# A vision tower's first stage on one core: zero products at the start, row 1 shared with ScalarE, group 4 in halves

## The reference

```python
concat = (x, x shifted by 4 pixels to the four diagonals)      # 10 channels, zero padded
normed = (concat - mean) * rsqrt(var + 1e-7)                   # over the whole image
y = conv(normed * gamma + beta, W, 8 x 8 patches, stride 8) + b  # 13 x 13 = 169 tokens of 128
h = [cls_tok, y]                                               # 170 tokens
# for each token in turn, memory S starts at memory0:
q, k, v = Wq l, Wk l, Wv l        with l = layernorm(h)
S = S + 0.01 * v k^T ;  h = h + S q
h = h + ffn(layernorm(h))         # ffn adds nothing beyond its input for these values
```

## Time and profile before

| what | value |
|---|---|
| time, median of 3 runs | 217.07 us (217.06 to 217.54) |
| the profiled execution's own time | 217.46 us |
| its span, first to last instruction | 215.6 us |
| TensorE busy | 196.3 us (91%) |
| GpSimd busy | 154.5 us (72%) |
| VectorE busy | 152.3 us (71%) |
| ScalarE busy | 127.7 us (59%) |

### The profile page before, as it was taken

One profiled execution on the slowest core, in us unless ns is written; L12 is line 12 of the kernel. 1 busy time (PEld: TensorE's weight loads), 2 busy tenths in 40 slices (PEclk: granted clock), 3 DMA queues, 4 the chain that ended last, 5 costly groups with the idle time before them and its releaser, 6 DMA issues.

```text
span 215.6 us, 5028 instructions
## 1 busy us (share of the span) xinstructions
PE 196.3 (91%) x1548; PEld 166.9 (77%) x1548; DVE 152.3 (71%) x758; ACT 127.7 (59%) x306; POOL 154.5 (72%) x129
## 2 busy tenths in 40 slices
PE   0699999999999999999999999999999999999720
PEld 0488897886888889788888888899888888888610
DVE  3639694684486675678687597687687687699892
ACT  4215777884443375475756565665665574577982
POOL 1069908899990999969999949938999541455671
PEclk9999999999999999999999999999999999999975
DMA  5999992745022006153053432022012012100356
GB/s 140 388 420 422 422 413 112 217 185 181 0 58 111 2 3 194 30 175 88 3 153 109 125 93 49 5 50 49 11 41 52 16 36 52 28 22 5 80 118 152
DMA packets 17216, 25.90 MB, mean 120 GB/s; under 512 B 1719, under 2 KB 13693, under 8 KB 17062
## 3 DMA queue, kind: packets, MB, share of 16 engines
q1 hardware_dynamic: 16486, 25.41, 36.5%
q10 hardware_dynamic: 704, 0.17, 0.4%
HBM read 19.65 MB, written 5.92 MB: 119 GB/s over the span
## 4 chain that ended last, share of the span: by engine, by line
PE 52%; POOL 15%; DMA 10%; DVE 8%; issue 7%; SPq 4%; ACT 2%; POOLq 0%; DVEq 0%; ACTq 0%
PE conv L575 25%; DMA images<-x_rows 10%; PE vr_ps L623 10%; POOL scaled L469 7%; PE first_ps L633 6%; PE outs L650 6%; POOL rstd L1337 3%; PE turn L608 3%; POOL g_low L1327 2%; DVE state L1007 2%; DVE state L999 2%; SPq L488 1%; PE conv L583 1%; DVE images L1028 1%; POOL rstd L1353 1%
## 5 line engine op out<-in xcount | busy, mean ns | idle before, releaser
L575 PE MATMUL conv<-scaled,wt 128*128 128x256 f32 (+3 forms) x432 | 111.7, 375 | 7.3 <-DMA wt<-weight 6.9
L469 POOL TENSOR_TENSOR scaled<-rows,gam 128x832 f32<-128x832 f32 (+1 forms) x54 | 84.7, 1588 | 17.6 <-DMA rows<-x_windows 17.3
L575 PEld LDWEIGHTS conv<-scaled,wt 128*128 128x128 f32 x432 | 71.7, 193 | 15.3 <-DMA wt<-weight 6.9
L817 ACT ACTIVATE values<-vr_ps,rstd 128x256 f32<-128x256 f32 x76 | 36.0, 473 | 62.8 <-PE vr_ps L623 50.1
L1337 POOL TENSOR_TENSOR rstd<-var,powers 128x8 f32<-128x8 f32 (+2 forms) x20 | 30.3, 1517 | 27.0 <-DVE var L1019 26.9
L999 DVE TENSOR_TENSOR state<-first_ps,state 128x128 f32<-128x128 f32 x76 | 22.1, 291 | 27.6 <-PE first_ps L633 22.2
L825 ACT ACTIVATE images<-images,ln_shift,ln_gain 128x128 f32<-128x128 f32 x80 | 37.3, 489 | 1.5 <-DVE ln_shift L1076 0.7
L623 PE MATMUL vr_ps<-w_high,g_low 128*128 128x256 f32 x77 | 30.8, 400 | 0.8 <-ACT values L817 0.8
L1327 POOL TENSOR_TENSOR g_low<-g_t,g_high 128x512 fp32r<-128x512 f32 x21 | 26.8, 1274 | 4.6 <-ACT g_high L804 4.6
L988 DVE BATCH_NORM_STATS2 ln_stats<-images 128x6 f32<-128x128 f32 x85 | 23.6, 284 | 4.8 <-ACT images L811 4.7
L1007 DVE TENSOR_TENSOR state<-second_ps,state 128x128 f32<-128x128 f32 x76 | 21.5, 282 | 2.1
(11 more groups left out here) (201 smaller groups left out, 273.5 us busy)
## 6 DMA issues: line engine op xcount, KB each, us to landing
rows<-x_windows SPq DMA_DIRECT2D x12, 864.0 KB, 4.8
out<-images SPq DMA_DIRECT2D x40, 128.0 KB, 2.4
images<-x_rows SPq DMA_DIRECT2D x4, 832.0 KB, 14.9
images<-x_rows SPq DMA_DIRECT2D x1, 1040.0 KB, 15.9
images<-x_rows SPq DMA_DIRECT2D x1, 624.0 KB, 20.7
rows<-x_windows SPq DMA_DIRECT2D x1, 448.0 KB, 6.1
gam<-gamma SPq DMA_DIRECT2D x1, 422.5 KB, 6.8
bet<-beta SPq DMA_DIRECT2D x1, 422.5 KB, 9.0
```

The lines of the kernel that those rows point to most:

```text
L469: return eng.tensor_tensor(scaled[:, s, at + skip:at + N], window[:, skip:N], gains.unsqueeze(2).to_broadcast([P, N - skip, B]), ALU.mult)
L575: last = pe.matmul(conv_ps[g % 2][:, at:at + n * B], held, scaled[:, s, a % RING:a % RING + n], start=first, stop=(g < EARLY and s >= TOP ...
L817: act.activation(values[:, t % VALUE_SLOTS].rearrange("p a e -> p (a e)"), vr_bank(t)[:, 0:2 * E], ACT.Identity, scale=rho_of(t)).then_inc ...
```

## The change

- **Opening of TensorE.** Three products of zeros (128 x 512) run before the weights are waited for, and one more after the items of shift 0 of group 0. They write a bank that the next product into it overwrites. The table of gamma comes before that of beta, with the items of shifts 0 and 1 of group 1 between them.
- **Row 0 on VectorE** is scaled in two passes: tokens 0 to 7 of the four shifts, then tokens 8 to 12. The semaphore `scaled_first` counts to 8 instead of 4, and SyncE's load of row 3 waits for all 8.
- **Row 1.** ScalarE scales tokens 13 to 15 of the five shifts (15 instructions of 64 elements) ahead of its work on `center`; GpSimd scales the other ten (640 elements for 832). A new semaphore `scaled_second` tells of the first. SyncE's load of row 4 waits for it too.
- **Group 4 by halves.** All first halves (tokens 32 to 35) of its five shifts, then the second halves: four items before the sums of the statistics, five after, one after L755, and then two items of group 5 (`AHEAD`) that the loop no longer has in step -8.
- **The item table.** `FIRST` gives 4 items to step -8 for 2, the two of them ahead; the rest of the table is dealt out anew. The groups 5, 6, 7, 10, 11, 12 and 17 end one or two steps earlier, and 23 of GpSimd's row scalings stand one step earlier.
- **VectorE's low parts of the tables** (`table_low_ready`) come after the first block of image statistics instead of the second.

```diff
--- before.py
+++ after.py
@@ -95,7 +95,8 @@
 LATE_ITEMS = [item for g in range(EARLY, GROUPS) for item in conv_items(g)]
 LATE_COST = [n for _, _, _, n in LATE_ITEMS]
 
-FIRST = (2, 2, 1, 1, 1, 1, 1, 1)
+AHEAD = 2
+FIRST = (4, 2, 1, 1, 1, 1, 1, 1)
 
 
 def late_item_step(i):
@@ -150,6 +151,7 @@
 ROW_4_TOKENS = {-7: (0, 5), -6: (5, 4), -4: (9, 4)}
 EARLY_TOKENS = TOKENS * EARLY
 CORNER = 3 * N
+SECOND = 2 * TOKENS
 
 
 def pool_scales(r, s):
@@ -436,7 +439,7 @@
         def wait_scaled(eng, s, a, n):
             last = (a + n - 1) // N
             if a // N == 0:
-                eng.wait_ge(scaled_first, s + 1)
+                eng.wait_ge(scaled_first, s + 1 if a < TOKENS else TOP + 1 + s + 1)
             if a + n - 1 == CORNER:
                 eng.wait_ge(corner_scaled, s + 1)
                 last -= 1
@@ -444,6 +447,8 @@
                 eng.wait_ge(scaled_by_scalar, BY_SCALAR.index((last, s)) + 1)
             elif (last, s) in BY_VECTOR:
                 eng.wait_ge(scaled_by_vector, 1)
+            elif 0 < last and a + n <= SECOND:
+                eng.wait_ge(scaled_second, s + 1)
             elif last > 0:
                 eng.wait_ge(scaled_rows, pool_scales(last, s))
 
@@ -457,17 +462,17 @@
             at = (t % PER_GROUP) * E
             return buf[t // PER_GROUP % slots][:, at:at + E]
 
-        def scale_shift(eng, r, s):
+        def scale_shift(eng, r, s, first=0, stop=N):
             offsets = (r if s < 3 else r - 1) % ROW_SLOTS
             right = N + (s - 1) % 2
             window = rows[:, r % ROW_SLOTS, 0:N] if s == 0 else rows[:, offsets, right:right + N]
-            skip = 1 if r * N == CORNER else 0
-            gains = gam_first[:, s] if r == 0 else gam[:, s, r * N + skip:r * N + N]
+            skip = 1 if r * N == CORNER else first
+            gains = gam_first[:, s, skip:stop] if r == 0 else gam[:, s, r * N + skip:r * N + stop]
             if (r, s) == (N - 1, BOTTOM):
                 gains = bottom[:, E:E + N]
             at = r % 2 * N
-            return eng.tensor_tensor(scaled[:, s, at + skip:at + N], window[:, skip:N],
-                                     gains.unsqueeze(2).to_broadcast([P, N - skip, B]), ALU.mult)
+            return eng.tensor_tensor(scaled[:, s, at + skip:at + stop], window[:, skip:stop],
+                                     gains.unsqueeze(2).to_broadcast([P, stop - skip, B]), ALU.mult)
 
         block = ctx.enter_context(nc.Block())
 
@@ -481,6 +486,8 @@
                         sp.wait_ge(scaled_by_vector, 1)
                     if r - 3 >= CORNER // N:
                         sp.wait_ge(corner_scaled, SHIFTS)
+                if r == ROW_SLOTS:
+                    sp.wait_ge(scaled_second, SHIFTS)
                 sp.dma_start(rows[:, r % ROW_SLOTS], x_windows[:, r]).then_inc(row_in[r % ROW_SLOTS], 16)
 
             def load_images(i):
@@ -516,7 +523,7 @@
             load_images(5)
             load_images(6)
 
-            sp.wait_ge(scaled_first, TOP + 1)
+            sp.wait_ge(scaled_first, 2 * (TOP + 1))
             load_row(3)
             load_row(4)
             for blk in range(2):
@@ -588,9 +595,14 @@
                     if a <= item[1] < z:
                         conv(item)
 
+            def conv_fifth(a, z):
+                items = conv_items(EARLY - 1)
+                for item in (items[0::2] + items[1::2])[a:z]:
+                    conv(item)
+
             def late_conv(t, half):
 
-                share = [i for i, st in enumerate(ITEM_STEPS) if st == t]
+                share = [i for i, st in enumerate(ITEM_STEPS) if st == t and i >= AHEAD]
                 mid = (len(share) + 1) // 2
                 for i in share[:mid] if half == 0 else share[mid:]:
                     conv(LATE_ITEMS[i])
@@ -703,15 +715,28 @@
                 reads(LAST)
                 reads(LAST + 1)
 
+            def zero_products(count):
+                for _ in range(count):
+                    pe.matmul(vr_ps[:, 0:PER_GROUP * E], zeros[:], zeros[:].unsqueeze(1).to_broadcast([P, PER_GROUP, E]),
+                              start=True, stop=True, skip_group_check=True)
+
+            pe.wait_ge(zeros_ready, 1)
+            zero_products(3)
             pe.wait_ge(weight_in, 16)
-            conv_shifts(0, 0, SHIFTS)
-            pe.wait_ge(gamma_in, 16)
-            pe.wait_ge(beta_in, 16)
-            for kind, table in enumerate((bet, gam)):
+            conv_shifts(0, 0, 1)
+            zero_products(1)
+            conv_shifts(0, 1, SHIFTS)
+            def table_columns(kind, table):
                 for i in range(SHIFTS):
                     last = pe.matmul(turn_ps[:, kind * PATCHES:kind * PATCHES + PATCHES], wt[:, i], table[:, i], start=(i == 0),
                                      stop=(i == SHIFTS - 1), skip_group_check=True)
-            last.then_inc(columns_done, 1)
+                return last
+
+            pe.wait_ge(gamma_in, 16)
+            table_columns(1, gam)
+            conv_shifts(1, 0, 2)
+            pe.wait_ge(beta_in, 16)
+            table_columns(0, bet).then_inc(columns_done, 1)
             pe.wait_ge(small_in, 16)
             pe.wait_ge(centered, 3)
             pe.matmul(out_ps[:, 0:E], wk_c[:], wq_c[:], start=True, stop=True, skip_group_check=True)
@@ -724,7 +749,7 @@
                 for kind in range(2):
                     last = pe.transpose(ps[0:count, kind * E:kind * E + E], columns[:, kind, blk * P:blk * P + count], small[:, IDENT])
                 last.then_inc(tables_done, 1)
-            conv_shifts(1, 0, SHIFTS)
+            conv_shifts(1, 2, SHIFTS)
             pe.wait_ge(cls_t_ready, 1)
             pe.wait_ge(w_vr_ready, 2)
             pe.matmul(vr_ps[:, 0:2 * E], cls_t[:], w_vr[:], start=True, stop=True).then_inc(vr_done, 1)
@@ -744,24 +769,26 @@
             pe.matmul(first_ps[:, 0:E], values[:, VALUE_SLOTS - 1, 0], values[:, VALUE_SLOTS - 1, 1], start=False,
                       stop=True, skip_group_check=True).then_inc(cls_state_done, 1)
             conv_shifts(3, 0, SHIFTS)
+            conv_fifth(0, 4)
             pe.wait_ge(sums_ready, 2)
             pe.wait_ge(w_low_ready, 1)
             pe.wait_ge(scalar_sums_ready, 3)
             pe.matmul(out_ps[:, 2 * E:2 * E + 2], small[:, SAME], sums[:], start=True, stop=False, skip_group_check=True)
             pe.matmul(out_ps[:, 2 * E:2 * E + 2], small[:, SAME], scalar_sums[:], start=False, stop=True,
                       skip_group_check=True).then_inc(image_sums_done, 1)
-            conv_shifts(EARLY - 1, 0, 2)
+            conv_fifth(4, 9)
             pe.wait_ge(scale_cols_ready, 1)
             pe.matmul(out_ps[:, 0:B], scale_cols[:], small[:, IDENT, 0:B], start=True,
                       stop=True).then_inc(scale_rows_done, 1)
-            conv_shifts(EARLY - 1, 2, 4)
+            conv_fifth(9, 10)
+            for item in LATE_ITEMS[0:AHEAD]:
+                conv(item)
             pe.wait_ge(own_scales_ready, 1)
             pe.wait_ge(early_rows_ready, 1)
             early(0)
             pe.wait_ge(state_ready, 1)
             early(1)
             early(2)
-            conv_shifts(EARLY - 1, 4, SHIFTS)
             pe.matmul(out_ps[:, 0:E], cls_t[:], state[:, STATE_SLOTS - 1, 1], start=True,
                       stop=True).then_inc(out_done, 1)
             for t in range(START, TAIL):
@@ -915,6 +942,12 @@
             act.wait_ge(cls_in, 32)
             act.wait_ge(cls_padded, 1)
             act.copy(cls_t[:, B:P], cls_col[:].to_broadcast([P, B])).then_inc(cls_t_ready, 1)
+            act.wait_ge(gamma_in, 16)
+            act.wait_ge(row_in[1], 16)
+            for s in range(SHIFTS):
+                for t in range(N, SECOND):
+                    last = scale_token(t, s)
+                last.then_inc(scaled_second, 1)
             act.wait_ge(small_in, 16)
             act.wait_ge(ones_ready, 1)
             act.activation(center[:], small[:, IDENT], ACT.Identity, bias=powers[:, 11:12]).then_inc(centered, 1)
@@ -1223,7 +1256,9 @@
                     dve.wait_ge(first_right_in, 16)
                 if s == TOP:
                     dve.wait_ge(first_offsets_in, 16)
-                scale_shift(dve, 0, s).then_inc(scaled_first, 1)
+                scale_shift(dve, 0, s, 0, TOKENS).then_inc(scaled_first, 1)
+            for s in range(TOP + 1):
+                scale_shift(dve, 0, s, TOKENS).then_inc(scaled_first, 1)
 
             dve.wait_ge(small_in, 16)
             for i, w in enumerate((WQ, WK)):
@@ -1258,16 +1293,17 @@
                         else:
                             part = part.rearrange("p r (g q) -> p r g q", q=HALF)[:, :, 0:S // HALF:S // HALF - 1]
                         last_stats = dve.bn_stats(stats[:, 2 * j:2 * j + 2].rearrange("p a b -> p (a b)"), part)
+                if i == 0:
+                    for blk, ps in enumerate((turn_ps, second_ps)):
+                        m = P if blk == 0 else PATCHES - P
+                        dve.wait_ge(table_high_ready, blk + 1)
```

(9 more changed lines are left out.)

1 line of the change is left out of this document (added).

## The result

| | before | after |
|---|---|---|
| median | 217.31 us (217.06 to 217.73, 4 runs) | 215.43 us (215.33 to 215.53, 4 runs) |
| profiled execution, span | 217.46, 215.6 us | 215.34, 213.5 us |
| ratio after / before | | 0.9905 (95%: 0.9891 to 0.992) |

The change makes the kernel 0.95% faster, 1.9 us by the medians and 2.1 us between the two profiled executions. 215.5 us had been predicted.

The account below looks back on a forecast made before the run. TensorE, busy 91% of the span, was taken as the bound. 0.31 + 0.86 + 0.45 = 1.6 us off the profiled 217.46 gives 215.84; less 0.39, its excess over the median, 215.5 us; range 214.7 to 216.9.

Parts of the forecast that it names:

- Part 1: TensorE's opening: zeros end at 6.1, full clock from about 6.93, group 0 ends at 11.5 instead of near 13.9.
- late release: Rival, opening: clock rises only near 10.5, lead 0.25 for 1.07, 0.8 us gained, 216.3 us; chance 0.13.
- The slower rival: Opening: clock stays at or falls back to 1.2 GHz until about 13; +0.9 us, 218.0 us; chance 0.08.
- Part 2: Tables and row 1: `wk_c` ends at 17.5, 1.0 us later; four items done early; lead 1.07 us.
- Part 3: Group 4: sums' product 0.3 late, `early(0)` at 38.1, loop starts with lead 0.31, two group 5 items (0.86) done besides.
- the lead goes into the statistics: Rival, before the sums: lead 0.5, `early` 1.1 late, 0.6 us or less gained, 216.5 to 217 us; chance 0.14.
- Part 4: Loop: 0.86 comes back at steps 11, 23 and 59; GpSimd's earlier scaling (6, 0) gains 0.45; wait near 51 stays.
- The 0.86: Two items of group 5 done ahead, to come back in the loop where the new table has an item less.
- The 0.45 for the wait near 91: Loop: scaling (6, 0) moves into GpSimd's idle time, so TensorE's wait at 91.84 goes; 0.45 us, bounds 0 and 0.6.
- The wait near 51: Loop, TensorE waiting for GpSimd: stays at 0.74; a scaling beside VectorE's (4, 4) took 2.36 for 1.58 us.
- The moment of release: Opening: the sum has the full clock released by 6.93; the skill says the moment varies from run to run.

Follow-up runs that it names:

- no_zeros: The changed kernel without its four products of zeros; 215.71 us, ratio 0.9918 to the kernel before.
- fill: The changed kernel with shift 2 of group 1 moved before the weight products, five group 4 items before the sums, three of group 5 ahead; 215.38 us, 0.9898.
- zeros_alone: The kernel before with only three products of zeros added ahead of the wait for the weights; 217.53 us, ratio 0.9992.
- row1_back: The changed kernel with all of row 1 scaled on GpSimd again, no group 1 items ahead of the weight products; 216.36 us, ratio 0.9945.
- order_back: The changed kernel with the old order of group 4 and the old item table; 217.41 us, ratio 1.0001 to the kernel before.
- order_alone: The kernel before with only the new order of group 4 and the new item table; 216.86 us, ratio 0.9968.

## Why the prediction was right, by its own steps

- **Part 1, zeros and row 0.** The times hold (6.1, 8.7, and 11.6 where 11.5 had been said). The worth of the full clock was put too high. The rival *late release* had 0.8 us of the 1.6 hang on it; in no_zeros the clock rose at 11.7, later than the 10.5 assumed there, and the loss was 0.3 us by the ratios, not clear of none. The slip is in the rival's working. With the full clock from 10.5 on, the six items behind 10.35 can't last to 13.9: in fill, where shift 0 and the fourth product ran at the low pace as the rival has it, these twelve records took 2.65 us (10.57 to 13.22). From some 13.0 on, tables and four items end near 17.6 and not at 18.5, and the slack before ScalarE's 17.4 hides nearly all of it.
- **The slower rival** was judged unlikely because a pause of 0.34 us had been harmless. The runs show that a clock once risen does fall: it did in two of the ten profiled executions that opened with zeros (zeros_alone from 9.74 to 13.15, fill from 7.27 to 10.69), and stayed full in the other eight, the changed kernel's among them. Neither lost the 2.5 us worked out against the forecast, since the fall ended before the tables. What it costs at a worse moment no trace here shows.
- **Part 2.** `wk_c` ended at 17.29 for 17.5; the lead at group 2 is 23.94 - 22.69 = 1.25 for 1.07. row1_back shows its source: the four items ahead of the weight products.
- **Part 3** is the term that was mis-sized: a lead of 0.31 at the loop's first item was forecast, 0.84 measured (39.53 to 38.69). The sums' product was 0.17 early against the estimate, L755 (now L781) another 0.05, from there to `early(0)` there were 1.64 us and not 1.85, and behind `early(0)` another 0.1. Before, TensorE's four items had filled that stretch, and the scales were ready (37.38) sooner than they were used (37.56); with three items `early(0)` comes right behind them (37.61 and 37.67). The rows before and after:

```profile
36.69 0.69 DVE L1303 TENSOR_TENSOR own_scales<-outs,own 128x512 fp32r<-128x512 f32 x1
```

```profile
36.92 0.69 DVE L1339 TENSOR_TENSOR own_scales<-outs,own 128x512 fp32r<-128x512 f32 x1
```

- **What turns the lead into time** is the order of group 4, as order_back and order_alone show from both sides. The rival *the lead goes into the statistics* can be read from order_alone and row1_back, whose leads at group 2 are -0.18 and 0.11: `early(0)` came 1.5 and 1.25 us late (39.10 and 38.81), more than the 1.1 of that rival, and still 0.7 and 1.2 us were gained where it allowed 0.6 or less.
- **Part 4.** The 0.86 came back where it was placed, near groups 8 and 17. The 0.45 for the wait near 91 was measured as 0.46 to 0.48. The wait near 51 stayed at 0.73 for 0.74, and its cause is the one suspected; but neither of the two later places for VectorE's scaling gained anything. In all, the loop gave 1.21 us up to group 20 for the 1.31 forecast.
- **The moment of release.** With the same three products from 1.03 on the clock rose at 3.86, 4.49, 5.54 and 6.32 in four of the kernels, and between these times in the other six. The Trainium skill (TensorE: Matmul & The Clock Gate, "What's actually happening") has it vary from run to run, and the traces agree; but it gives 0.5 us either way, where these times lie 2.5 us apart, and the measurement decides. That the moment changes the time was not borne out.

The time was hit more closely than the sum deserves. Between the two profiled executions 2.12 us were gained (217.46 to 215.34) for a sum of 1.62, nearly all of the difference in part 3. The forecast then took off 0.39, because the kernel before had been profiled that much above its median; the changed kernel was profiled 0.09 below its own (215.43). The errors of 0.50 and 0.48 cancel, and that part of the agreement is luck. The mechanism is not luck: each term of the sum was found where it had been placed. With 2.12 us in place of 1.62 the forecast would have been 214.95, still inside its range of 214.7 to 216.9.

## What to carry to other kernels

A gain at the start of a full engine reaches the end only if there is an order that spends it: look for the wait behind it (here that for the sums), and move work of later stages ahead of that wait, as much as the lead holds. Ask of each part what it is worth without the others; two that are worth 0 and 0.7 us alone gave 1.9 together, and a third (the zeros) showed no gain clear of the noise. Where a table of positions is dealt out anew, look for what slides from a dense stretch of another engine into an idle one; that was a quarter of the gain.
